# The first 128 keys of phase attention through a state, and one column chunk of each image pair turned by GpSimd

## The reference, cut to what matters

```python
key_phase = jnp.tanh(x @ Wk + bk) * pi          # [B, L, 32] = 4 sets x 8 planes
query_phase = jnp.tanh(x @ Wq + bq) * pi
V = x @ Wv + bv
for s in range(N_SETS):
    bound = key_ph[:, :, s, :, None] * V[:, :, None, :]
    memory = jnp.cumsum(bound, axis=1)
    retrieved = (memory * jnp.conj(qry_ph[:, :, s, :, None])).sum(axis=2).real
    total = total + weights[s] * retrieved
...
total = gate * total + (1.0 - gate) * pos_contrib
return x + total / sqrt(positions * 8) @ Wo + bo
```

## Time and profile before

| | |
|---|---|
| median of 3 runs | 1647.76 us (1645.76 to 1649.63) |
| profiled execution | 1646.93 us |
| its span in the trace | 1644.2 us |
| TensorE busy | 89% of the span |
| VectorE busy | 87% |
| ScalarE busy | 76% |
| GpSimd busy | 62% |

### The profile page before, as it was taken

How to read it: one execution, slowest core, us unless ns; L and a number is a source line. 1 busy time by engine, 2 the same in 40 slices (tenths; PEclk the granted TensorE clock), 3 DMA queues, 4 the chain that set the end, 5 groups by cost and what they waited for, 6 DMA issues and landing times.

```text
span 1644.2 us, 30506 instructions
## 1 busy us (share of the span) xinstructions
PE 1455.5 (89%) x9030; PEld 1121.5 (68%) x9030; DVE 1432.7 (87%) x5763; ACT 1246.3 (76%) x2190; POOL 1012.6 (62%) x857
## 2 busy tenths in 40 slices
PE   2689999999999999999999999999999972776671
PEld 1467777777777777777777777777777751555551
DVE  3369999999999999999999999999999983886661
ACT  2799999999999999999999999999999741111110
POOL 0116666666666666666666666666666665788887
PEclk9899999999999999999999999999999996998885
DMA  9977777777777777777677777777776102676653
GB/s 170 245 157 151 147 145 145 141 143 133 129 124 127 123 121 120 121 123 116 120 120 120 117 117 119 119 121 121 117 119 113 39 19 65 101 117 105 94 82 34
DMA packets 257947, 195.67 MB, mean 119 GB/s; under 512 B 59000, under 2 KB 237275, under 8 KB 257784
## 3 DMA queue, kind: packets, MB, share of 16 engines
q1 hardware_dynamic: 216280, 175.30, 59.6%
q0 software_dynamic: 39296, 17.55, 8.7%
q10 hardware_dynamic: 2208, 0.89, 0.4%
HBM read 84.28 MB, written 83.73 MB: 102 GB/s over the span
## 4 chain that ended last, share of the span: by engine, by line
PE 75%; POOL 10%; issue 5%; DVE 4%; DMA 3%; ACT 3%; SPq 1%; POOLq 0%; DVEq 0%
PE bank L896 12%; POOL out_rows L640 9%; PE bank L966 8%; PE bank L949 7%; PE bank L1037 6%; PE bank L1046 5%; PE bank L920 5%; PE bank L934 4%; PE bank L904 4%; PE bank L1053 3%; PE bank L1022 2%; PE bank L985 2%; PE bank L1012 2%; PE bank L1008 2%; PE bank L1002 2%
## 5 line engine op out<-in xcount | busy, mean ns | idle before, releaser
L596 POOL DMA_INDIRECT slot_rows<-xs,slot x640 | 648.9, 1014 | 447.4 <-DVE slot L1382 278.0
L657 ACT ACTIVATE img<-img 84x980 f32<-84x980 f32 x190 | 340.5, 1793 | 13.7 <-DMA img<-in_x 7.1
L896 PE MATMUL bank<-img,w_tok 126*128 126x392 f32 (+1 forms) x640 | 228.1, 504 | 29.2 <-DMA img<-img 23.7
L640 POOL DMA_INDIRECT out_rows<-img,etok x128 | 198.7, 1552 | 54.9 <-issue 36.1
L580 POOL TENSOR_TENSOR rs<-ve,neg_half 128x12 f32<-128x12 f32 (+1 forms) x66 | 150.0, 2273 | 111.2 <-DVE ve L1265 111.2
L896 PEld LDWEIGHTS bank<-img,w_tok 126*128 126x128 f32 (+1 forms) x640 | 124.0, 195 | 115.2 <-issue 23.9
L949 PEld LDWEIGHTS bank<-pos_a,v 128*128 128x128 f32 x768 | 139.8, 190 | 42.6
L727 ACT ACTIVATE xs<-h,nb,rs 128x128 f32<-128x128 f32 x384 | 154.1, 481 | 2.5 <-DVE nb L1271 2.5
L949 PE MATMUL bank<-pos_a,v 128*128 128x325 f32 (+2 forms) x768 | 155.7, 338 | 0.0
L740 ACT ACTIVATE xh<-h,nb,rs 128x128 f32<-128x128 f32 x384 | 154.0, 480 | 0.6 <-DVE nb L1271 0.6
L966 PE MATMUL bank<-a_t,v 128*128 128x325 f32 (+2 forms) x768 | 150.3, 345 | 0.6 <-DVE a_t L1325 0.6
(11 more groups left out here) (196 smaller groups left out, 3581.6 us busy)
## 6 DMA issues: line engine op xcount, KB each, us to landing
img<-in_x SPq DMA_DIRECT2D x384, 150.1 KB
img<-img SPq DMA_DIRECT2D x254, 160.8 KB
img<-img SPq DMA_DIRECT2D x128, 128.6 KB
out_rows<-fin SPq DMA_DIRECT2D x128, 128.0 KB
slot_rows<-xs,slot POOLq DMA_INDIRECT x640
slot_rows<-init_rows SPq DMA_DIRECT2D x16, 540.0 KB, 8.9
img<-slot_rows SPq DMA_DIRECT2D x32, 270.0 KB
h<-in_txt SPq DMA_DIRECT2D x64, 128.0 KB
```

Source lines behind the costliest of these rows:

```text
L596: g.indirect_dma_start(out=slots_d, out_offset=bass.IndirectOffsetOnAxis(ap=slot[0:nt, q.x, part, r:r + 1], axis=0), in_=xs[0:nt, q.x, par ...
L640: g.indirect_dma_start(out=out, out_offset=bass.IndirectOffsetOnAxis(ap=etok[:, q.load, m:m + 1], axis=0), in_=ysum[:, q.load, m, :], in_o ...
L657: a.activation(cols[:, b0:b0 + nb, :], raw[:, q.u, :].rearrange("p (t b) -> p b t", b=P)[:, b0:b0 + nb, :], ACT.Copy)\
L896: ins = mm(bank[:, 5, 0:2 * PATCHES], w_tok[r, m, :], xk[r, k.u, :, m, :], start=(m == 0), stop=(m == SHIFT - 1))
```

## The change

The first 128 keys are taken out of the masked scores for all queries behind them. For rows 128 to 324, what these keys give is q_l times one 64 x 128 state, the product of the first 128 keys and their values:

- `keys` transposes the first tile of keys of both images on TensorE, ScalarE copies it to `kt` (`key_rows`), `first_state` makes the state of each image (two matmuls with 64 output rows, 128 columns), and ScalarE copies it to `state` (`state_rows`).
- `scores` has 128, 197 and 69 columns instead of 325, 197 and 69, and one VectorE instruction masks all 394.
- VectorE multiplies the queries of rows 128 to 324 by the norm (`scaled_queries`, 197 columns, into `qn`).
- `phase_out` has 128, 197 and 69 columns for each image, and adds for each a matmul of `state` with `qn` (64 rows of the array, 197 columns). One semaphore, `pe_ta`, is set for both images at its end.
- `transpose_1` waits for `a_st` too, since it writes the bank where the state was.
- The constants grow by `maskp` (394 columns) and `norm` (197).

The copy of the chunk of 784 columns goes from ScalarE to the head of GpSimd's body, for all pairs from the third on; for the second pair ScalarE keeps it. GpSimd's step k turns pair k-2 and scatters pair k-8.

```diff
+SCORES = [(0, TILE), (TILE, L), (2 * TILE, L)]
+AT = [0, TILE, L, L + BELOW[2]]
...
+    put("maskp", np.concatenate([m0[:, 0:TILE], m1, m2], 1) * np.concatenate([invn[:, a:b] for a, b in SCORES], 1))
+    put("norm", np.repeat(invn[:, TILE:L], 128, 0))
...
@@ GpSimd
+            def turn_columns_2(q):
+
+                wait_dma(pool, s_xin, q, 2 * C)
+                wait_dma(pool, s_spread[2], q, 2, 1)
+                b0, nb = CHUNKS[2]
+                g.tensor_copy(cols[:, b0:b0 + nb, :], raw[:, q.u, :].rearrange("p (t b) -> p b t", b=P)[:, b0:b0 + nb, :])\
+                    .then_inc(S["a_d2"], 1)
...
             def body(k):
+                p2 = k.back(2)
...
+                if p2.runs():
+                    turn_columns_2(p2)
                 if p8.runs():
                     ready(p8)
                     scatter(p8, 0)
@@ ScalarE
             def early(q, n):
-                return (q.c, n) in ((0, 2), (0, 1), (0, 0))
+                return q.c == 0 or n == 2 and q.c > 1
...
+            def key_rows(y):
+                act.wait_ge(S["pe_kt"], y.count())
+                a.activation(kt[:, :], bank[:, 7, 0:TILE], ACT.Copy).then_inc(S["a_kt"], 1)
+            def state_rows(y):
+                act.wait_ge(S["pe_st"], y.count())
+                a.activation(state[:, :], bank[:, 2, 0:D], ACT.Copy).then_inc(S["a_st"], 1)
...
                     if not early(n1, 1):
                         turn_columns_1(n1)
+                if p2.runs():
+                    key_rows(p2)
                 if p1.runs():
                     normal_1(p1)
+                if p2.runs():
+                    state_rows(p2)
@@ TensorE
-            def scores(y):
+            def keys(y):
                 pe.wait_ge(S["a_qs"], y.count())
                 pe.wait_ge(S["v_w"], y.count())
+                tr(bank[:, 7, 0:TILE], kq[:, y.u, 0, 0:TILE], ident).then_inc(S["pe_kt"], 1)
+            def scores(y):
                 wait(pe, S["a_sl"], y, 2)
                 for i, (t0, _) in enumerate(TILES):
                     for s in range(2):
                         r = slice(64 * s, 64 * s + 64)
-                        b = (6, 1)[s]
-                        at = 0 if i < 2 else BELOW[1]
-                        dst = bank[:, b + (i > 0), at:at + BELOW[i]]
-                        ins = mm(dst, kq[r, y.u, 0, t0:t0 + TILE], kq[r, y.u, 1, i * TILE:L], start=(i < 2), stop=(i != 1),
-                                 skip_group_check=True)
+                        a0, a1 = SCORES[i]
+                        ins = mm(bank[:, (6, 1)[s], AT[i]:AT[i + 1]], kq[r, y.u, 0, t0:t0 + TILE], kq[r, y.u, 1, a0:a1],
+                                 start=(i == 0), stop=(i == NT - 1), skip_group_check=True)
                 ins.then_inc(S["pe_sc"], 1)
+            def first_state(y):
+                pe.wait_ge(S["a_kt"], y.count())
+                for s in range(2):
+                    ins = mm(bank[64 * s:64 * s + 64, 2, 0:D], kt[:, 64 * s:64 * s + 64], v[:, y.u, s, 0, :], start=True, stop=True)
+                ins.then_inc(S["pe_st"], 1)
...
-            def phase_out(y, s):
-                flat = a_t[:, s].rearrange("p a l -> p (a l)")
-                for i in range(NT):
-                    ins = mm(bank[:, 6 + s, i * TILE:L], v[:, y.u, s, i, :], flat[:, BEGIN[i]:BEGIN[i + 1]],
-                             start=(i == 0), stop=(i == NT - 1))
-                ins.then_inc(S[f"pe_ta{s}"], 1)
...
+            def phase_out(y):
                 pe.wait_ge(S["v_ma"], y.count())
-                phase_out(y, 0)
...
+                for s in range(2):
+                    flat = a_t[:, s].rearrange("p a l -> p (a l)")
+                    for i in range(NT):
+                        a0, a1 = SCORES[i]
+                        mm(bank[:, 6 + s, a0:a1], v[:, y.u, s, i, :], flat[:, AT[i]:AT[i + 1]],
+                           start=(i == 0), stop=False, skip_group_check=True)
+                pe.wait_ge(S["a_st"], y.count())
+                for s in range(2):
+                    r = slice(64 * s, 64 * s + 64)
+                    ins = mm(bank[:, 6 + s, TILE:L], state[r, :], qn[r, :], start=False, stop=True, skip_group_check=True)
+                ins.then_inc(S["pe_ta"], 1)
...
             def transpose_1(k):
                 pe.wait_ge(S["a_xh"], k.count())
                 wait(pe, S["v_mb"], k, 1)
+                wait(pe, S["a_st"], k, 1)
...
                 if p2.runs():
+                    keys(p2)
                     scores(p2)
                 if p4.runs():
                     counts(p4)
+                if p2.runs():
+                    first_state(p2)
+                if p4.runs():
                     shared_out(p4)
@@ VectorE
+            def scaled_queries(y):
+                dve.wait_ge(S["a_qs"], y.count())
+                TT(qn[:, :], kq[:, y.u, 1, TILE:L], cst("norm"), ALU.mult)
             def mask(y, s, done, b):
-                TT(a_t[:, s, 0, :], bank[:, b, 0:L], cst("maskn")[:, 0:L], ALU.mult)
-                n = BELOW[1] + BELOW[2]
-                TT(a_t[:, s, 1, 0:n], bank[:, b + 1, 0:n], cst("maskn")[:, L:], ALU.mult).then_inc(S[done], 1)
+                flat = a_t[:, s].rearrange("p a l -> p (a l)")
+                TT(flat[:, 0:AT[NT]], bank[:, b, 0:AT[NT]], cst("maskp"), ALU.mult).then_inc(S[done], 1)
...
             def weigh_sets(y):
-                dve.wait_ge(S["pe_ta1"], y.count())
+                dve.wait_ge(S["pe_ta"], y.count())
...
                     residual_bias(p2)
+                    scaled_queries(p2)
```

More of the change, by code:

```diff
@@ L66 @@
 for _n, _w in (("ident", 128), ("pos", L), ("tok", 2 * NT), ("sel", SETS), ("query", 1), ("key", 1), ("delta", 2), ("dpos", 1),
-               ("dump", 4), ("empty", 8), ("absent", 2 * NT), ("below", 128), ("maskn", BEGIN[NT]), ("iota", CAP)):
+               ("dump", 4), ("empty", 8), ("absent", 2 * NT), ("below", 128), ("maskn", BEGIN[NT]), ("maskp", AT[NT]), ("norm", BELOW[1]),
+               ("iota", CAP)):
     CONST[_n] = (_at, _at + _w)
@@ L284, in program @@
         kq = sb("kq", [128, 2, 3, L])
+        kt = sb("kt", [128, 128])
+        state = sb("state", [128, D])
+        qn = sb("qn", [128, BELOW[1]])
         v = sb("v", [128, 2, 2, NT, D])
@@ L379, in program @@
         s_spread = [sems(f"s_spread{n}") for n in range(COPIES)]
-        names = """pe_tok pe_th pe_tx pe_k pe_v pe_g pe_sc pe_pf pe_pa0 pe_pa1 pe_ta0 pe_ta1 pe_tx2 pe_f1a  pe_lgt  pe_f3b pe_lg pe_wo pe_o
+        names = """pe_tok pe_th pe_tx pe_k pe_v pe_g pe_kt pe_st pe_sc pe_pf pe_pa0 pe_pa1 pe_ta pe_tx2 pe_f1a  pe_lgt  pe_f3b pe_lg pe_wo pe_o
             v_ht  v_st1 v_mm v_dd v_vs v_ve v_nb v_v v_ma v_mb v_w v_u v_tot v_hb  v_h2 v_st2
@@ L383, in program @@
               v_sg  v_sinv
-            a_d0 a_d1 a_d2 a_h a_xh a_xt a_th a_abs a_sin a_qs a_g a_x2 a_x2t a_lgt a_sl a_lg a_small
+            a_d0 a_d1 a_d2 a_h a_xh a_xt a_th a_abs a_sin a_kt a_st a_qs a_g a_x2 a_x2t a_lgt a_sl a_lg a_small
             p_rs""".split()
@@ L960, in position_out_1 @@
                 position_out(y, 1)
-            def phase_out(y, s):
-                flat = a_t[:, s].rearrange("p a l -> p (a l)")
-                for i in range(NT):
-                    ins = mm(bank[:, 6 + s, i * TILE:L], v[:, y.u, s, i, :], flat[:, BEGIN[i]:BEGIN[i + 1]],
-                             start=(i == 0), stop=(i == NT - 1))
-                ins.then_inc(S[f"pe_ta{s}"], 1)
-            def phase_out_0(y):
-                pe.wait_ge(S["v_ma"], y.count())
-                phase_out(y, 0)
-            def phase_out_1(y):
-                phase_out(y, 1)
+            def phase_out(y):
+                pe.wait_ge(S["v_ma"], y.count())
+                for s in range(2):
[9 more added lines that the diff above has]
+                ins.then_inc(S["pe_ta"], 1)
             def transpose_2(z):
@@ L1089, in body @@
                 if p2.runs():
-                    phase_out_0(p2)
-                    phase_out_1(p2)
+                    phase_out(p2)
                 if p3.runs():
```

## The result

The changed kernel takes 1677.88 us (median of 4 runs, 1675.44 to 1681.81), the kernel before 1647.65 in the same runs: ratio 1.0186, interval [1.0162, 1.0209]. It is 30 us slower; 21 were forecast. 1677.88 lies inside the range, and near the upper end of the likeliest case's own 1658 to 1680.

The account below looks back on a forecast made before the run. The prediction took TensorE to set the 20.00 us period, VectorE having only 0.4 us to spare. +0.37 us a pair over 59 periods (+22.1), -2.4 and +1.5 in the ramp gave +21: 1668 us, range 1626 to 1684.

Parts of the forecast that it names:

- the likeliest case: The forecast itself: new split matmuls pay borders, 0.55 to 0.9 us a pair, giving 1658 to 1680 us; chance 0.58.
- four border prices: TensorE: entering and leaving `first_state` (0.15 + 0.19 us) and the state matmuls (0.26 + 0.11), beyond their columns.
- The rival with free borders: TensorE switches to split matmuls without a gap; the pair gains 0.34 us, giving 1626 us; chance 0.22.
- VectorE: TensorE hides all of it: VectorE in the loop: 197 fewer columns gain 0.26 us a pair, which does not show while TensorE sets the pace.
- GpSimd's copy costs nothing in the loop: The chunk's copy, 1.53 us at the head of GpSimd's body, ends at 822.8 us and makes no engine late.
- The rival that had 6 in 100: GpSimd's copy holds VectorE's `ssum` up by 1.2 us; period some 20.7 us, time 1687 us; chance 0.06.
- The copy's start: GpSimd's copy needs the six loads, issued from 808.23 to 811.6 us and landed by about 821.3 at the latest.
- The 0.9 us of slack towards `rs`: GpSimd: after the copy ends at 822.8 us, 0.9 us remain before `rs`, and VectorE's `nb` behind it, would be late.
- The ramp: Start of the run: ScalarE's saved copies give -2.4 us for three pairs; larger constants cost +1.5 us (0 to 1.8).
- The sum: Whole run: 22.1 - 2.4 + 1.5 = +21 us on the profiled 1646.93 us, giving 1668 us.

Follow-up runs that it names:

- fs_next: `attn_only` with one move, `first_state` ahead of `counts`, directly behind `scores`; 1658.35 us, ratio 1.0071 to the kernel before.
- copy_only: The kernel before with only GpSimd's copy of the 784-column chunk added, attention unchanged; 1672.54 us, ratio 1.0159 to the kernel before.
- old_turn_later: `copy_only` with GpSimd turning each chunk one step later and SP spreading it just ahead of the last chunk's; 1692.67 us, ratio 1.0275.
- spread_first: The changed kernel with SP issuing the 784 chunk's spread before the six loads; 1675.64 us, ratio 1.0169 to the kernel before.
- attn_only: The changed kernel with the 784-column chunk copy given back to ScalarE for all pairs; 1677.17 us, ratio 1.0179 to the kernel before.

## Why the prediction was right, and where it was not

- **TensorE sets the pace and the pair costs 0.37 us more, four border prices against 0.34 us of saved columns.** Right. Every line came out within 0.07 us of its figure (`first_state` 0.37, `shared_out` 1.53, `phase_out` 1.51, `transpose_2` 0.72, state matmuls 0.53); the sum is 0.42 (0.04 of it in `counts`, which the prediction left out). `fs_next` shows the price by removal. The rival with free borders is out.
- **"VectorE: TensorE hides all of it" and GpSimd's copy costs nothing in the loop.** This is the step that failed. The rival that had 6 in 100 took place beside the forecast one: VectorE is held 0.92 us a pair. It cost less than the 0.7 us a period of that rival, since part of it fell into the slack, but `copy_only` shows 24 us for it alone. My argument against it, two copies side by side in the setup, was no evidence: one instance, of two copies that began together; why VectorE's ran undisturbed stays open. The rival itself looked only at `ssum`, at 819.69. The copy's latest window by the prediction's own sum, 821.3 to 822.8, held `over`, `slotf` and the gate weights in the trace before:

```profile
822.47 0.17 DVE L1376 TENSOR_SCALAR over<-xs 128x12 f32<-128x12 f32 x1
```

That the time came out in the range although this term was put at nothing is in part luck: it adds only 0.09 us a period to TensorE's own 0.44, because the two overlap. The trace before held better evidence that I did not read: `hi` and `xs` (`tensor_scalar`) took 298 and 292 ns on average beside GpSimd's scatters, `over`, with no scatter beside it, 174:

```profile
L1439 DVE TENSOR_SCALAR hi<-top 128x12 f32<-128x12 f32 x30 | 8.9, 298 | 0.0
L1376 DVE TENSOR_SCALAR over<-xs 128x12 f32<-128x12 f32 x30 | 5.2, 174 | 0.0
```

`hi` was long (over 0.2 us) in 20 of these 30 pairs, those in which it began more than 0.51 us behind the scatter's start, and ended within 0.02 us of the scatter's end.
The Trainium skill, page SBUF — State Buffer, section SBUF: two separate sides, states that GpSimd and VectorE share a port pair which one instruction holds to its end. These runs agree: with two SBUF operands `residual` took 2.33 us instead of 0.94 and `ssum` 1.02 on average in `old_turn_later` instead of 0.15, and `over`, one operand, ended 0.03 us after the copy. `places`, a reduction, kept its 0.94 us, though the copy began 0.14 us behind its start.
- **The copy's start.** Its input was taken to be the six loads, landed by 821.3. GpSimd waited 2.1 us, for the spread of the pair before it, which SP issues behind those loads; in `spread_first`, where it waited for the loads alone, the copy starts 0.8 us earlier on average. In the changed kernel it starts 5.5 us behind the first matmul of `scores` (4.0 to 6.8) where at most 4.8 had been taken (821.3 - 816.47). That delay was not foreseen, but the forecast's own window would have met `over` too. The 0.9 us of slack towards `rs` held: VectorE waited for `rs` once from 200 to 1300 us, 0.3 us.
- **The ramp.** -2.4 + 1.5 us was forecast, -4.3 measured. `copy_only` has -3.9, `attn_only` +3.2; the start of the third `token` alone differs by 3 us between kernels whose setups are equal (65.25 in the changed kernel, 67.96 in `spread_first`; 68.16 in `attn_only`, 65.29 in `fs_next`), so the size of the constants' share is open.
- **The sum.** Forecast +22.1 - 0.9. Measured between the spans: +30.5 in 58 periods, -4.3, +3.2. The 0.53 is 0.44 of TensorE's own (`attn_only`) and 0.09 of VectorE's.

## What to carry to other kernels

Count a matmul on part of the array with its borders: here 0.15 to 0.26 us to enter and 0.11 to 0.19 to leave, so that 0.34 us of saved columns became 0.42 us of loss; put split groups side by side before you add one. Before you give GpSimd work, list VectorE's instructions in its window and look for one of two SBUF operands or a `tensor_scalar`; it waits for the end of GpSimd's instruction, on an engine whose slack may lie elsewhere in the period. Parts with separate prices do not add where two engines are nearly equal: 29 and 24 us gave 30.

## What was not expected of the hardware

An instruction of 12 elements (`over`) took up to 1.56 us, and one of 64 bf16 columns 2.27 us, beside a GpSimd copy of 1.5 us that began 0.64 us after it. Cutting that copy in four left the sum of VectorE's waits at 0.92 us. From a stretch with the rows split straight to one with the columns split TensorE paid 0.16 us, no more than from the full array.
